# Gated cross attention on one core: the next chunk's summaries and row transposes placed ahead of the current chunk's output projection

## Chip, cores and metric

One core of a Trainium2 chip runs the whole program in one launch. The metric is the device time in microseconds. The kernel before was timed three times: 2039.60, 2035.11 and 2036.13 us, median 2036.13.

## What is computed

The program is a two-layer transformer over x of shape (8, 256, 512) with context of the same shape, float32. Four blocks follow each other: a gated long convolution, a routed mixture of experts, a gated linear cross attention, and a soft mixture of experts. The change lies in the third block alone. Cut to what matters, that block is:

```
q    = feature(layernorm(x) @ Wq.T)           # per head of 32 columns, 16 heads
gate = sigmoid(layernorm(x) @ Wg.T + bg)
k, v = split(ctx @ Wkv.T);  k = feature(k)    # feature(t) = t + 1 if t > 0 else exp(t)
kv   = sum over the 256 tokens of k^T v ;  k_sum = sum of k
attn = (q @ kv) / (q . k_sum + 1e-6)
x    = x + tanh(g) * ((attn * gate) @ Wo.T)
```

## The kernel before, in words

The 2048 tokens are cut into four chunks (NCH = 4) of 512 tokens. A chunk is four tiles of 128 tokens, and two batch entries of 256 tokens. Every float32 operand of a matmul is split into a float16 high part and a float16 low part, and one product is three matmuls (hi*hi, hi*lo, lo*hi), issued by `three` (L1470 to L1474). The work of a chunk c is cut into steps, each of which names the part that every engine plays in it:

- TC, TX (n = 0 to 3): TensorE transposes tile n of the context (TC) or of the normalised rows (TX) into a PSUM bank (L1478). ScalarE copies it out as the high part (L1304, L1310), VectorE makes the low part (L1406).
- CB: VectorE adds the two gathered expert rows to x (L1383, L1386) and takes the layer norm's statistics. NA is the variance and ScalarE's square root (L115), NB the reciprocal (L108) and the normalised rows (L1400).
- K, V: 12 matmuls of 512 columns each. For K, VectorE takes min(., 0) (L1368) and ScalarE the exponential (L1319). For V, ScalarE makes the high part (L1325), VectorE the low part (L1417). KF is the rest of K's feature: VectorE writes `feat` (L1375), ScalarE its high part (L1328), GpSimd its low part (L1281). GpSimd then issues the two gathers of tile n of chunk c + 1.
- Q, G, QF (n = 0 to 3): the same for the queries (L1331, L1344, L1286) and the gate (L1338, L1427), 12 matmuls each for Q and G.
- SM (n = 0 to 3): 12 matmuls each for the key-value summaries, out of all four K and V tiles of the chunk. TensorE waits for the low parts of all four (L1511). VectorE masks the sums (L1434). SS (n = 0, 1) splits them (L1347 on ScalarE, L1439 on VectorE).
- AT (n = 0 to 7): six matmuls of 256 columns. VectorE then takes denominator, reciprocal and product (L1447, L1450, L1455), ScalarE the high part (L1354), GpSimd the low part (L1290).
- OUT (n = 0 to 3): 12 matmuls, which wait for the low parts of AT 0 to 3 or AT 0 to 7 (L1533). VectorE adds the result to the rows (L1459), and SyncE stores them.

One list, `schedule`, holds the steps of all chunks in an order written out by hand (L1194 to L1200). Each of TensorE, VectorE, ScalarE and GpSimd walks this same list and plays its part of each step, so each engine's queue has the list's order, and a step that waits holds everything behind it on that engine. `mixed(a, b)` merges two lists evenly. In the kernel before the order for a chunk is: Q, G, QF of c mixed with TC, CB of c + 1; NA of c + 1; SM and SS of c; NB of c + 1; K, V, KF of c + 1 mixed with the eight AT of c; OUT of c mixed with TX of c + 1. The middle mix comes out as K0 AT0 V0 AT1 KF0, K1 AT2 V1 AT3 KF1, K2 AT4 V2 AT5 KF2, K3 AT6 V3 AT7 KF3. In front of the loop stand, for chunk 0, the transposes, the weights' splits (WS, L1314 and L1411), and K, V, KF mixed with WS and TX.

PSUM is a ring of eight banks, handed out in the list's order. A step that takes a bank waits until the step that used it eight uses earlier has been read (L1482 to L1486). SyncE's queue (L1221 to L1246) loads the context and the weights in eight pieces, then per chunk c: context and rows of c + 1, and then the four stores of chunk c, each behind its `out_read`.

Of the kernel before, what the change touches and what calls it, by code (L numbers as in the profile page):

```python
# [21 lines left out]
KD = D // P  # L22
CH = 4 * P
NCH = T // CH
# [27 lines left out]
def mixed(a, b):  # L52

    at = [((i + 0.5) / len(a), 0, o) for i, o in enumerate(a)] + [((i + 0.5) / len(b), 1, o) for i, o in enumerate(b)]
    return [o for _, _, o in sorted(at, key=lambda v: v[:2])]
# [1065 lines left out]
def xattn_phase(nc, k, x1s, y_rows, ctx, wq_t, wg_t, bg_cols, wkv_t, wo_t, x3):  # L1121
# [3 lines left out]
    with phase(nc) as st:  # L1125
# [8 lines left out]
        ctx_in, x2 = sb("a_ctx", [P, 4, D]), sb("a_x2", [P, X_BUFS, 4, D])  # L1134
# [20 lines left out]
        ctx_loaded, x_loaded = sem("a_ctx_loaded"), [sem(f"a_x_loaded{u}") for u in range(X_BUFS)]  # L1155
        y_loaded = [sem(f"a_y_loaded{u}") for u in range(4)]
        first_added, combined, normed = sem("a_first_added"), sem("a_combined"), sem("a_normed")
        c_turned, c_hi, c_lo = sem("a_c_turned"), sem("a_c_hi"), sem("a_c_lo")
        x_turned, x_hi, x_lo = sem("a_x_turned"), sem("a_x_hi"), sem("a_x_lo")
        k_done, v_done, q_done, g_done, gate_done = (sem(f"a_{n}") for n in ("k_done", "v_done", "q_done", "g_done", "gate_done"))  # L1160
        sum_done, mix_done, out_done, out_read = (sem(f"a_{n}") for n in ("sum_done", "mix_done", "out_done", "out_read"))
        v_hi_done, low_done, low_exp_done = sem("a_v_hi_done"), sem("a_low_done"), sem("a_low_exp_done")
        feat_done, feat_hi, feat_lo = sem("a_feat_done"), sem("a_feat_hi"), sem("a_feat_lo")
# [5 lines left out]
        x1s_d, x3_d, ctx_d = (a.rearrange("(c k p) d -> p (c k) d", p=P, k=4) for a in (x1s, x3, ctx))  # L1169
# [3 lines left out]
        NP = len(pieces)  # L1173

        def staged(n):
            cols = pieces[n][1][0].shape[2]
            return stage[:, n % 2, :, 0:cols]
# [6 lines left out]
        def ops(c, op, count):  # L1184
            return [(c, op, n) for n in range(count)] if c < NCH else []

        def projections(c, first, second, last, count):

            return [(c, op, n) for n in range(count) for op in (first, second, last)] if c < NCH else []

        def weights(first, end):
            return [(0, "WS", n) for n in range(first, end)]

        schedule = (ops(0, "TC", 4) + weights(0, 2) + ops(0, "CB", 4) + ops(0, "NA", 1) + ops(0, "NB", 1)  # L1194
                    + mixed(projections(0, "K", "V", "KF", 4), weights(2, 4) + ops(0, "TX", 4) + weights(4, NP)))
        for c in range(NCH):
            schedule += mixed(projections(c, "Q", "G", "QF", KD), [o for n in range(4) for o in ((c + 1, "TC", n), (c + 1, "CB", n)) if c + 1 < NCH])
            schedule += ops(c + 1, "NA", 1) + ops(c, "SM", 4) + ops(c, "SS", 2) + ops(c + 1, "NB", 1)
            schedule += mixed(projections(c + 1, "K", "V", "KF", 4), ops(c, "AT", 2 * KD))
            schedule += mixed(ops(c, "OUT", 4), ops(c + 1, "TX", 4))  # L1200


        READ = {"TC": (c_lo, 4), "TX": (x_lo, 4), "K": (feat_done, 8), "Q": (feat_done, 8), "V": (v_lo_done, 4), "G": (gate_exp, 4),
# [13 lines left out]
        def run(step):  # L1217
            for at in schedule:
                step(*at, home.get(at))

        @block.sync  # L1221
        def _(sp):
            def load_rows(c):
                if c >= X_BUFS:

                    sp.wait_ge(stored, (c - X_BUFS + 1) * 4 * 16)
                sp.dma_start(x2[:, c % X_BUFS], x1s_d[:, c * 4:c * 4 + 4, :]).then_inc(x_loaded[c % X_BUFS], 16)

            sp.dma_start(ctx_in[:, :, :], ctx_d[:, 0:4, :]).then_inc(ctx_loaded, 16)
            sp.dma_start(bg[:, :], bg_cols).then_inc(small_loaded, 16)  # L1230
            for n, (m, dst, b) in enumerate(pieces):
                if n >= 2:
                    sp.wait_ge(w_lo, n - 1)
                sp.dma_start(staged(n), m[b * P:(b + 2) * P, :].rearrange("(k p) n -> p k n", p=P)).then_inc(w_loaded[n % 2], 16)
                if n == 1:
                    load_rows(0)
            for c in range(NCH):
                if c < NCH - 1:

                    sp.wait_ge(c_turned, 4 * c + 4)  # L1240
                    sp.dma_start(ctx_in[:, :, :], ctx_d[:, c * 4 + 4:c * 4 + 8, :]).then_inc(ctx_loaded, 16)
                    load_rows(c + 1)
                for t in range(4):
                    sp.wait_ge(out_read, c * 4 + t + 1)
                    sp.dma_start(x3_d[:, c * 4 + t, :], x2[:, c % X_BUFS, t]).then_inc(stored, 16)
            sp.wait_ge(stored, NCH * 4 * 16)  # L1246
# [47 lines left out]
        @block.scalar  # L1294
        def _(act):
            A = nc.scalar.activation

            def step(c, op, n, bank):
                if op == "TC":
                    act.wait_ge(c_turned, c * 4 + n + 1)  # L1300
                    if c:

                        act.wait_ge(v_done, c * 4)
                    A(ct[0][:, :, n * P:(n + 1) * P], ring[:, bank, :].rearrange("p (k i) -> p k i", i=P), ACT.Copy).then_inc(c_hi, 1)  # L1304
                if op == "TX":
                    act.wait_ge(x_turned, c * 4 + n + 1)
                    if c:

                        act.wait_ge(g_done, c * 4)
                    A(xt[0][:, :, n * P:(n + 1) * P], ring[:, bank, :].rearrange("p (k i) -> p k i", i=P), ACT.Copy).then_inc(x_hi, 1)  # L1310
                if op == "WS":
                    act.wait_ge(w_loaded[n % 2], (n // 2 + 1) * 16)
                    _, dst, b = pieces[n]
                    A(dst[0][:, b:b + 2, :], staged(n), ACT.Copy).then_inc(w_hi, 1)  # L1314
                if op == "NA":
                    ln.root(nc, act, c)
                if op == "K":
                    act.wait_ge(low_done, c * 8 + n + 1)
                    A(low_exp[:, n % 2, :], low[:, n % 2, :], ACT.Exp).then_inc(low_exp_done, 1)  # L1319
                if op == "V":  # L1320
                    act.wait_ge(v_done, c * 4 + n + 1)
                    if c:

                        act.wait_ge(sum_done, c * 4)
                    A(v_hi[:, n, :, 0:P], ring[:, bank, :].rearrange("p (m i) -> p m i", i=P), ACT.Copy).then_inc(v_hi_done, 1)  # L1325
                if op == "KF":
                    act.wait_ge(feat_done, c * 8 + n + 1)
                    A(k_hi[:, n, :], feat[:, n % 2, :], ACT.Copy).then_inc(feat_hi, 1)  # L1328
                if op == "Q":
                    act.wait_ge(low_done, c * 8 + n + 5)  # L1330
                    A(low_exp[:, n % 2, :], low[:, n % 2, :], ACT.Exp).then_inc(low_exp_done, 1)  # L1331
                if op == "G":
                    act.wait_ge(g_done, c * 4 + n + 1)
                    if c:

                        act.wait_ge(denom_done, c * 8)

                    A(gate[:, n, :], ring[:, bank, :], ACT.Exp, bias=bg[:, n:n + 1], scale=-1.0).then_inc(gate_exp, 1)  # L1338
                if op == "QF":
                    act.wait_ge(feat_done, c * 8 + n + 5)  # L1340
                    if c:

                        act.wait_ge(mix_done, c * 8)
                    A(q_hi[:, n, :], feat[:, n % 2, :], ACT.Copy).then_inc(feat_hi, 1)  # L1344
                if op == "SS":
                    act.wait_ge(kv_done, c * 4 + n * 2 + 2)
                    A(kv_hi[:, n], kv[:, n], ACT.Copy).then_inc(kv_hi_done, 1)  # L1347
                if op == "AT":
                    b, m = divmod(n, KD)
                    act.wait_ge(weighted_done, c * 8 + n + 1)  # L1350
                    if c:

                        act.wait_ge(out_done, c * 4)
                    A(a_hi[:, m, b * N:(b + 1) * N], weighted[:, n % 2, :], ACT.Copy).then_inc(a_hi_done, 1)  # L1354
            act.wait_ge(small_loaded, 16)
            act.wait_ge(bg_negated, 1)
            run(step)

        @block.vector
# [107 lines left out]
        def _(pe):  # L1467
# [13 lines left out]
            def step(c, op, n, bank):  # L1481
# [26 lines left out]
                if op == "SM":  # L1508
# [5 lines left out]
                    for q in range(2):  # L1514
                        m = half * 2 + q
# [7 lines left out]
                if op == "AT":  # L1523

                    b, m = divmod(n, KD)
                    pe.wait_ge(feat_lo, c * 8 + 8)
                    pe.wait_ge(kv_lo_done, c * 2 + b + 1)
                    qs = [a[:, m, b * N:(b + 1) * N] for a in (q_hi, q_lo)]
                    for o in range(2):
                        last = three(ring[:, bank, o * N:(o + 1) * N], [a[:, b, m, o, :] for a in (kv_hi, kv_lo)], qs, True, True)  # L1530
                    last.then_inc(mix_done, 1)
                if op == "OUT":
                    pe.wait_ge(a_lo_done, c * 8 + (n // 2 + 1) * 4)  # L1533
                    pe.wait_ge(w_lo, NP)
                    for m in range(KD):
                        last = three(ring[:, bank, :], [a[:, m, n * P:(n + 1) * P] for a in (a_hi, a_lo)],
                                     [a[:, m, :] for a in wo], m == 0, m == KD - 1)
                    last.then_inc(out_done, 1)
            run(step)


# [686 lines left out]
```

## Time and profile before

| | us |
|---|---|
| median of three runs (2035.11 to 2039.60) | 2036.13 |
| the profiled execution's own time | 2038.1 |
| its span, first to last instruction | 2036.3 |
| cross attention in it, first transpose to last output matmul | 832.1 to 1173.6 |
| mean granted TensorE clock over the span | 0.924 |

The span is the time from the first to the last instruction, and the profiled execution's own time has about 2 us around it. All starts in the rows further down are microseconds from the start of the span. A group of 12 matmuls is shown as 12 overlapping rows: a row's duration (0.38 us for 512 columns) is longer than the distance between two starts (about 0.22 us), since matmuls are pipelined. The granted clock is a share of full speed, where 1.00 is 2.4 GHz and 0.50 is 1.2 GHz.

### The profile page before, as it was taken

How to read it: one execution, taken by the hardware profiler on the slowest of the kernel's cores; microseconds unless marked ns; L12 is line 12 of the kernel's file. 1: busy time of each engine (PE TensorE's matmuls, PEld its weight loads, DVE VectorE, ACT ScalarE, POOL GpSimd, SP SyncE). 2: the span in 40 equal slices, each digit the busy share in tenths (PEclk: the TensorE clock that was granted, in tenths of full speed). 3: DMA queues.
4: the chain of work that ended last, by engine and by line, in shares of the span. 5: the costliest groups of instructions: out<-in, count | busy, mean ns of one | idle time of the engine just before them, and what ended most of it. 6: DMA issues, size and time to landing. Idle time of an engine off the chain costs nothing. (4 is left out here: it accounts for less than half of the span.)

```text
span 2036.3 us, 29066 instructions
## 1 busy us (share of the span) xinstructions
PE 1699.5 (83%) x10248; PEld 1006.8 (49%) x10249; DVE 1141.6 (56%) x2234; ACT 716.2 (35%) x1366; POOL 419.4 (21%) x324
## 2 busy tenths in 40 slices
PE   2989948999279999588988736798989898989898
PEld 2778823444146666344544413454545454545454
DVE  4978843332643333576868646646465655556463
ACT  2322113333222222242333225735454443535352
POOL 1323303333411110233222113501010101010100
PEclk6999979999689999789999868899999899999999
DMA  8222233333422222433020052200000000000000
GB/s 179 62 74 86 86 119 107 119 119 99 134 68 84 82 82 68 185 104 103 13 92 21 11 176 66 90 1 32 1 32 0 31 0 31 0 31 0 21 13 20
DMA packets 78734, 134.52 MB, mean 66 GB/s; under 512 B 6626, under 2 KB 31202, under 8 KB 78514
## 3 DMA queue, kind: packets, MB, share of 16 engines
q1 hardware_dynamic: 71488, 113.45, 17.4%
q0 software_dynamic: 5680, 18.62, 3.2%
q10 hardware_dynamic: 1474, 1.21, 0.2%
q8 instruction: 59, 0.97, 0.2%
q14 instruction: 33, 0.27, 0.0%
HBM read 101.98 MB, written 31.28 MB: 65 GB/s over the span
## 5 line engine op out<-in xcount | busy, mean ns | idle before, releaser
L2041 PE MATMUL s_ring<-w_mu_hi,s_xt_hi 128*128 128x512 f16 x256 | 104.7, 409 | 45.7 <-DVE s_xt_lo L1948 45.7
L1953 DVE TENSOR_REDUCE s_top<-s_lg 128x1 f32<-128x512 f32 x64 | 43.8, 685 | 130.5 <-ACT s_lg L1855 130.5
L463 PE MATMUL ring<-prod_hi,toep 128*128 128x288 f16 x320 | 93.0, 291 | 18.2 <-DVE terms L383 10.1
L274 POOL TENSOR_TENSOR prod_lo<-prod,prod_hi 128x2304 f16<-128x2304 f32 x16 | 73.2, 4576 | 166.9 <-ACT prod_hi L307 156.6
L2025 DVE TENSOR_TENSOR s_g_lo<-s_ring,s_g_hi 128x512 f16<-128x512 f32 x64 | 43.4, 689 | 109.9 <-ACT s_g_hi L1897 109.9
L2042 PE MATMUL s_ring<-w_mu_lo,s_xt_hi 128*128 128x512 f16 x256 | 104.4, 408 | 0.0
L2043 PE MATMUL s_ring<-w_mu_hi,s_xt_lo 128*128 128x512 f16 x256 | 103.8, 405 | 0.0
L1800 POOL TENSOR_TENSOR s_h_lo<-s_h,s_h_hi 128x512 f16<-128x512 f32 x32 | 36.9, 1154 | 311.7 <-DVE s_h_hi L2022 311.7
L1794 POOL TENSOR_TENSOR s_xln<-s_xln,s_gamma 128x512 f32<-128x512 f32 x16 | 21.7, 1376 | 372.2 <-DVE s_xln L1934 372.2
L2041 PE MATMUL s_ring<-w_w_hi,s_xt_hi 128*128 128x512 f16 x256 | 98.0, 383 | 0.0
L2042 PE MATMUL s_ring<-w_w_lo,s_xt_hi 128*128 128x512 f16 x256 | 98.0, 383 | 0.0
L2043 PE MATMUL s_ring<-w_w_hi,s_xt_lo 128*128 128x512 f16 x256 | 97.8, 382 | 0.0
L2041 PE MATMUL s_acc<-w_w_hi,s_g_hi 128*128 128x512 f16 x256 | 97.1, 379 | 0.0
L2042 PE MATMUL s_acc<-w_w_lo,s_g_hi 128*128 128x512 f16 x256 | 97.0, 379 | 0.0
L2043 PE MATMUL s_acc<-w_w_hi,s_g_lo 128*128 128x512 f16 x256 | 97.0, 379 | 0.0
L464 PE MATMUL ring<-prod_lo,toep 128*128 128x288 f16 x320 | 93.0, 291 | 0.0
L465 PE MATMUL ring<-prod_hi,toep 128*128 128x288 f16 x320 | 93.0, 290 | 0.0
L2006 DVE TENSOR_TENSOR s_xw_lo<-s_ring,s_xw_hi 128x512 f16<-128x512 f32 x64 | 44.1, 689 | 73.0 <-ACT s_xw_hi L1889 73.0
L1855 ACT ACTIVATE s_lg<-s_ring,s_rs 128x512 f32<-128x512 f32 x64 | 44.0, 688 | 115.8 <-PE s_ring L2043 115.8
L380 DVE TENSOR_TENSOR terms<-ring,q_e 128x512 f32<-128x512 f32 x64 | 66.8, 1044 | 27.3 <-PE ring L465 25.0
L1087 DVE TENSOR_TENSOR e_h<-e_up,e_silu 128x352 f32<-128x352 f32 x39 | 20.4, 524 | 109.3 <-ACT e_silu L1066 109.3
L991 POOL DMA_INDIRECT e_rows<-normed_rows,slot_token x39 | 37.0, 950 | 197.6 <-PE e_turn L1005 181.7
(396 smaller groups left out, 4919.2 us busy)
## 6 DMA issues: line engine op xcount, KB each, us to landing
expert_rows<-e_y SPq DMA_DIRECT2D x39, 256.0 KB, 2.0
toep<-ssm_split SPq DMA_DIRECT2D x14, 512.0 KB, 5.1
stage<-in_L_ffn_gate_w SPq DMA_DIRECT2D x8, 704.0 KB
stage<-in_L_ffn_up_w SPq DMA_DIRECT2D x8, 704.0 KB
c_rows<-in_ctx SPq DMA_DIRECT2D x8, 512.0 KB, 10.3
x_rows<-in_x SPq DMA_DIRECT2D x8, 512.0 KB
res<-in_x SPq DMA_DIRECT2D x128, 32.0 KB
after_conv<-gated SPq DMA_DIRECT2D x128, 32.0 KB
```

Of the source, the lines that this page charges most:

```text
L274: nc.gpsimd.tensor_tensor(prod_lo[:, u].rearrange("p k e r -> p (k e r)"), prod[:, u, :], prod_hi[:, u].rearrange("p k e r -> p (k e r)"), ...
L380: nc.vector.tensor_tensor(to(0, (9, 4), (1, 8)), values(0, (8, 4), (1, 8)), weights(0, (0, 4), (1, 8)), ALU.mult)
L463: nc.tensor.matmul(out, w_hi, hi, start=(n == 0), stop=False)
L464: nc.tensor.matmul(out, w_hi, lo, start=False, stop=False)
L465: last = nc.tensor.matmul(out, w_lo, hi, start=False, stop=(n == m))
L1855: A(lg[:, t, j * D:(j + 1) * D], ring[:, bank, :], ACT.Copy, scale=rs[:, t:t + 1]).then_inc(S["lg_out"], 1)
L1953: V.tensor_reduce(top[:, t, j:j + 1], lg[:, t, j * D:(j + 1) * D], AX.X, ALU.max).then_inc(S["top_done"], 1)
L2006: V.tensor_tensor(xw[1][:, t, j * D:(j + 1) * D], ring[:, bank, :], xw[0][:, t, j * D:(j + 1) * D], ALU.subtract).then_inc(S["xw_lo"], 1)
L2025: V.tensor_tensor(g[1][:, n % G_BUFS, :], ring[:, bank, :], g[0][:, n % G_BUFS, :], ALU.subtract).then_inc(S["g_lo"], 1)
L2041: mm(out_, a[0], b_[0], start=first, stop=False)
L2042: mm(out_, a[0], b_[1], start=False, stop=False)
L2043: return mm(out_, a[1], b_[0], start=False, stop=last_)
```

## The change

The steps are the same and so are the instructions of each. What differs is their order in the list, two waits, and SyncE's order.

- For chunk 0, SM and SS stand in front of the loop, behind K, V, KF, where they stood behind Q, G, QF of chunk 0.
- In the loop, behind Q, G, QF of c, come NA, K0, V0 and NB of c + 1. Then the other ten steps of K, V, KF of c + 1 are mixed with AT of c. This comes out as KF0 AT0, K1 AT1 V1 AT2 KF1 AT3, K2 V2 AT4 KF2 AT5, K3 AT6 V3 AT7 KF3. Then SM 0 to 3, TX 0 to 3 and SS 0, 1 of c + 1, and last OUT 0 to 3 of c.
- In the last chunk the order behind Q, G, QF is AT0 to AT4, OUT0, AT5, AT6, OUT1, AT7, OUT2, OUT3.
- TensorE's wait of AT asks for the low part of its own column block of the queries and no longer for all four. ScalarE's SS waits until the AT steps of the chunk before have read the summaries.
- SyncE issues the loads of context and rows of chunk c + 2 ahead of the stores of chunk c. Those of chunk 1 stand where they stood, behind the weights.

```diff
         schedule = (ops(0, "TC", 4) + weights(0, 2) + ops(0, "CB", 4) + ops(0, "NA", 1) + ops(0, "NB", 1)
-                    + mixed(projections(0, "K", "V", "KF", 4), weights(2, 4) + ops(0, "TX", 4) + weights(4, NP)))
+                    + mixed(projections(0, "K", "V", "KF", 4), weights(2, 4) + ops(0, "TX", 4) + weights(4, NP))
+                    + ops(0, "SM", 4) + ops(0, "SS", 2))
         for c in range(NCH):
             schedule += mixed(projections(c, "Q", "G", "QF", KD), [o for n in range(4) for o in ((c + 1, "TC", n), (c + 1, "CB", n)) if c + 1 < NCH])
-            schedule += ops(c + 1, "NA", 1) + ops(c, "SM", 4) + ops(c, "SS", 2) + ops(c + 1, "NB", 1)
-            schedule += mixed(projections(c + 1, "K", "V", "KF", 4), ops(c, "AT", 2 * KD))
-            schedule += mixed(ops(c, "OUT", 4), ops(c + 1, "TX", 4))
+            if c + 1 < NCH:
+                schedule += ops(c + 1, "NA", 1) + projections(c + 1, "K", "V", "KF", 4)[:2] + ops(c + 1, "NB", 1)
+                schedule += mixed(projections(c + 1, "K", "V", "KF", 4)[2:], ops(c, "AT", 2 * KD))
+                schedule += ops(c + 1, "SM", 4) + ops(c + 1, "TX", 4) + ops(c + 1, "SS", 2) + ops(c, "OUT", 4)
+            else:
+                at, out = ops(c, "AT", 2 * KD), ops(c, "OUT", 4)
+                schedule += at[:KD] + mixed(at[KD:], out[:2]) + out[2:]
...
+            def load_chunk(c):
+                sp.wait_ge(c_turned, 4 * c)
+                sp.dma_start(ctx_in[:, :, :], ctx_d[:, c * 4:c * 4 + 4, :]).then_inc(ctx_loaded, 16)
+                load_rows(c)
+
+            load_chunk(1)
             for c in range(NCH):
-                if c < NCH - 1:
-
-                    sp.wait_ge(c_turned, 4 * c + 4)
-                    sp.dma_start(ctx_in[:, :, :], ctx_d[:, c * 4 + 4:c * 4 + 8, :]).then_inc(ctx_loaded, 16)
-                    load_rows(c + 1)
+                if c + 2 < NCH:
+                    load_chunk(c + 2)
...
                 if op == "SS":
                     act.wait_ge(kv_done, c * 4 + n * 2 + 2)
+                    if c:
+
+                        act.wait_ge(mix_done, c * 8)
...
                 if op == "AT":
 
                     b, m = divmod(n, KD)
-                    pe.wait_ge(feat_lo, c * 8 + 8)
+                    pe.wait_ge(feat_lo, c * 8 + 4 + m + 1)
                     pe.wait_ge(kv_lo_done, c * 2 + b + 1)
```

## Rows read from the trace of the kernel before

**Rows 1.** Timeline, TensorE: start us, us, engine, line, op, out<-in, count, [idle before <-releaser]
```profile
906.90 0.27 PE L1519 MATMUL a_ring<-a_v_hi,a_k_hi 128*128 128x256 f16 x1
...
960.20 0.38 PE L1472 MATMUL a_ring<-a_xt_hi,wq_hi 128*128 128x512 f16 x1 [1.46 <-issue]
...
965.64 0.87 PE L1478 MATMUL a_ring<-ident,a_ctx 128*128 128x128 f32 x3 [2.69 <-DMA a_ctx<-in_ctx]
...
986.88 0.27 PE L1519 MATMUL a_ring<-a_v_hi,a_k_hi 128*128 128x256 f16 x1
...
991.27 0.38 PE L1472 MATMUL a_ring<-wkv_hi,a_ct_hi 128*128 128x512 f16 x1
...
1022.17 0.39 PE L1472 MATMUL a_ring<-wo_hi,a_a_hi 128*128 128x512 f16 x1 [1.34 <-DVE a_feat L1375]
...
1025.21 0.38 PE L1472 MATMUL a_ring<-wo_hi,a_a_hi 128*128 128x512 f16 x1
...
1030.82 0.38 PE L1472 MATMUL a_ring<-wo_hi,a_a_hi 128*128 128x512 f16 x1 [2.42 <-DVE a_feat L1375]
...
1038.49 0.38 PE L1472 MATMUL a_ring<-a_xt_hi,wq_hi 128*128 128x512 f16 x1 [1.46 <-issue]
...
1116.57 0.38 PE L1472 MATMUL a_ring<-a_xt_hi,wq_hi 128*128 128x512 f16 x1 [1.46 <-issue]
...
1137.28 0.27 PE L1519 MATMUL a_ring<-a_v_hi,a_k_hi 128*128 128x256 f16 x1
```

**Rows 2.** Timeline, VectorE, chunk 1 after its last gate group, same columns
```profile
990.32 1.00 DVE L104 TENSOR_TENSOR x_var<-x_gap,x_spread 128x4 f32<-128x4 f32 x1
...
995.98 0.17 DVE L108 RECIPROCAL x_rstd<-x_std 128x4 f32<-128x4 f32 x1
...
998.62 0.42 DVE L1447 SCALAR_TENSOR_TENSOR a_denom<-a_ring,a_gate 128x256 f32<-128x256 f32 x1
...
1002.24 0.69 DVE L1417 TENSOR_TENSOR a_v_lo<-a_ring,a_v_hi 128x512 f16<-128x512 f32 x1 [0.97 <-ACT a_v_hi L1325]
...
1029.44 0.68 DVE L1375 SCALAR_TENSOR_TENSOR a_feat<-a_ring,a_low_exp 128x512 f32<-128x512 f32 x1
```

**Rows 3.** Timeline, ScalarE, same stretch and columns
```profile
991.36 0.20 ACT L115 ACTIVATE x_std<-x_var 128x4 f32<-128x4 f32 x1
...
994.82 1.28 ACT L1319 ACT_TABLE_LOAD   x1
...
1001.63 0.58 ACT L1325 ACTIVATE a_v_hi<-a_ring 128x512 f16<-128x512 f32 x1
```

**Rows 4.** Timeline, GpSimd, chunk 1, last K tile
```profile
1030.86 1.16 POOL L1281 TENSOR_TENSOR a_k_lo<-a_feat,a_k_hi 128x512 f16<-128x512 f32 x1
```

**Rows 5.** Timeline, GpSimd and TensorE, before the first Q and G groups end
```profile
883.88 1.16 POOL L1281 TENSOR_TENSOR a_k_lo<-a_feat,a_k_hi 128x512 f16<-128x512 f32 x1 [5.54 <-ACT a_k_hi L1328]
...
884.21 0.66 PE L1478 MATMUL a_ring<-ident,a_ctx 128*128 128x128 f32 x2 [7.44 <-DMA a_ctx<-in_ctx]
```

**Rows 6.** Windows: PE, PEld, DVE, ACT, POOL busy us (count), PEclk, DMA share, GB/s
```profile
832.10:834.50 2.40, 2.35 (x11) 2.35 (x12) 0.65 (x2) 0.94 (x2) 1.79 (x3) 0.50 1.02 418
...
835.20:836.00 0.80, 0.41 (x3) 0.17 (x2) 0.64 (x2) 0.76 (x2) 0.66 (x1) 0.96 1.03 415
...
884.20:890.00 5.80, 5.79 (x16) 2.59 (x17) 3.48 (x5) 0.80 (x2) 2.75 (x3) 0.51 0.65 219
...
1156.50:1159.60 3.10, 3.09 (x8) 1.14 (x9) 3.03 (x4) 0.42 (x1) 0.67 (x1) 0.51 0.00 0
```

**Rows 7.** Timeline, VectorE, GpSimd and TensorE, last chunk
```profile
1144.83 0.42 DVE L1447 SCALAR_TENSOR_TENSOR a_denom<-a_ring,a_gate 128x256 f32<-128x256 f32 x1
...
1147.41 0.41 DVE L1447 SCALAR_TENSOR_TENSOR a_denom<-a_ring,a_gate 128x256 f32<-128x256 f32 x1
...
1148.02 0.67 POOL L1290 TENSOR_TENSOR a_a_lo<-a_mixed,a_a_hi 128x256 f16<-128x256 f32 x1 [8.10 <-ACT a_a_hi L1354]
...
1173.22 0.38 PE L1474 MATMUL a_ring<-wo_hi,a_a_lo 128*128 128x512 f16 x1
```
## The prediction

> **What bounds the kernel now.** I read the page first, then the timelines of TensorE and VectorE over the cross attention, and last the windows for the granted clock. TensorE's timeline [rows 1] shows a repeating period: from Q0 of one chunk to Q0 of the next are 960.20 to 1038.49 = 78.3 us and 1038.49 to 1116.57 = 78.1 us. Small waits stand in it: 2.69 us for the context (its load is queued behind the stores), 1.34 us before OUT0, 2.42 before OUT2, 1.46 before Q0. Most name VectorE. VectorE's timeline [rows 2] shows why. From its first AT (998.62) to KF3 (1029.44) it needs 30.8 us for 8 AT, 4 V, 3 K and 3 KF (KF0 to KF2), and idles only where V waits for ScalarE's copy, 0.97 us each. TensorE's same stretch, K0 to OUT0, is 991.27 to 1022.17, 30.9 us with its waits inside [rows 1]. So between the last G and the last low part VectorE sets the pace. TensorE hides two OUT and two TX groups under VectorE's last steps (OUT0 starts 7.3 us before KF3's feature), and only 1038.49 - 1030.82 = 7.7 us of the chunk follow when AT7 is ready.
>
> **Chunks 1 to 3 in the new order.** I walk the list from the first instant after G3 (986.88 in chunk 1 [rows 1]), called G.
> - SM leaves this place: 991.27 - 986.88 = 4.4 us of TensorE, the mask and split of VectorE too. But VectorE's next steps are K0, V0, NB, KF0, and they wait for ScalarE. The square root starts at 991.36 and takes 0.20 [rows 3], behind VectorE's variance [rows 2]; nothing moves it. The table load behind it takes 1.28 [rows 3], so K0's exponential starts at G + 6.0. That pass and V0's copy take about 0.6 each (the copy's row has 0.58 [rows 3]), V0's low part starts at G + 7.2 and takes about 0.6 [rows 2]. NB and one 512-column pass took 998.62 - 995.98 = 2.64 [rows 2]; NB and KF0 take as much. So the first AT starts on VectorE at G + 10.5, where it started at 998.62 - 986.88 = G + 11.7. Thus 4.4 us less work in front is worth 1.2 us.
> - From the first AT to KF3's feature: 30.8, less V0 (0.97 + 0.6) and KF0 (0.6) already done, plus about 0.3 because V2 now follows K2 directly and ScalarE must make exponential and copy in turn. That is 28.9 us, so KF3's feature starts at G + 39.4. AT's relaxed wait on TensorE buys nothing, as VectorE reaches each AT later than TensorE.
> - SM of the next chunk now waits for KF3's low part: GpSimd starts it 1.42 us behind the feature (1029.44 to 1030.86 [rows 2, 4]) and takes 1.16 [rows 4]. **SM starts at G + 42.1.** TensorE has finished AT7 by G + 30.9 (the K0 to OUT0 stretch of before, waits and all), so it idles over 11 us, at one place, with four TX and two ready OUT groups queued behind SM.
> - After it TensorE still has SM 4.4 us, and four OUT and four TX, 1025.21 - 1022.17 = 3.04 us a pair [rows 1], 12.2 us. VectorE has little to do then, so nothing else waits.
> - The clock: before OUT0 of the last chunk TensorE idled over 7 us and then ran at a granted 0.51 (1.2 GHz) for 3.1 us; after a like wait for the context the low stretch was 5.8 us [rows 6]. Half of the low time is lost: 1.55 to 2.9 us. For 11 to 13 us of idling I take 2.1 us, nearer the last chunk's because no transfer or PSUM wait is mixed in; the ends are 0 (the clock happens to be up) and 2.9.
>
> G to the next Q0 is then 42.1 + 4.4 + 12.2 + 2.1 = 60.8 us. Q0 to G3 is 20.7 us without transposes (1116.57 to 1137.28 [rows 1]) and four TC add 4 x 0.45 (a pair less an eighth of 20.7), 22.5 us in all. The context load of chunks 2 and 3 stands ahead of the stores and needs only TC3 of the chunk before, some 60 us earlier, so its wait goes entirely, with the low clock behind it. SyncE's moved row load of chunk 3 waits for chunk 0's stores, long done; the 32 gathers of GpSimd keep their places behind KF, and KF3's stand behind the low part that SM needs.
>
> Sums: chunk 0's G to Q0 was 53.3 (906.90 to 960.20 [rows 1]), now 60.8: **+7.5**. The two full periods were 78.3 and 78.1, now 83.3: **+5.0 and +5.2**.
>
> **Chunk 0 in front of the loop.** SM(0) must wait for KF3(0)'s low part, 883.88 + 1.16 [rows 5]: start 885.1. Before, Q0 had run inside the 7.44 us wait for the context, whose place in SyncE's queue is unchanged, TC0 started at 884.21 [rows 5] and G0 ended at 890.0, all at 0.51 [rows 6]. Now SM 4.4 + 2.1 for the clock, Q0 2.6, TC0 0.45 and G0 2.6 end at 897.2: **+7.2**.
>
> **The last chunk.** Without SM and SS in front, VectorE's first AT starts at about G + 1.3 (when the gate of QF3 is done), 1138.6 for 1144.83 [rows 7]. Each AT takes 1147.41 - 1144.83 = 2.58, and its low part ends 3.86 after its start (1148.02 + 0.67 - 1144.83 [rows 7]). OUT0 starts at 1138.6 + 3 x 2.58 + 3.86 = 1150.2, at the low clock, and ends at 1154.4. VectorE, in order, waits for it from 1151.5, so interleaving costs 3.1 us there. With OUT0's and OUT1's pass (0.65 each) AT7 starts at 1161.0, its low part ends at 1164.9, and OUT2, OUT3 (5.2 + 1.55 for the clock) end at 1171.6 instead of 1173.6 [rows 7]: **-2.0**.
>
> Total: 7.5 + 5.0 + 5.2 + 7.2 - 2.0 = **+22.9 us**. The soft mixture behind it is only shifted. The profiled execution would take 2038.1 + 22.9 = 2061.0; it lay 2.0 above the median of 2036.13, so I predict 2059.0. Its own range: with the clock up at all four SM starts 8.4 less, with 2.9 at each 3.2 more, and 1 us either way for each of the four starts: 2046.6 to 2066.2.
>
> **A rule against this change.** Transposes now stand in a block of 16 between SM and OUT. In this trace 16 transposes alone ran at 0.50, and at 835.2, with nothing else behind or beside them, the granted clock was 0.96 [rows 6]: transposes raised it. The Trainium skill says the opposite (TensorE: Matmul & The Clock Gate, Part 4: PE-mode transpose): the full clock does not engage for transposes, since they do not count as busy in the same way. This trace disagrees with it. I keep it as a rival.
>
> **The rivals.**
> - Transposes do not hold the clock: OUT0 behind the TX block runs at 1.2 GHz too, 2.6 us more for each of three blocks, 2059.0 + 7.8 = 2066.8. Against it is the row at 835.2. Chance 0.07.
> - The change does not do what it says for the loads: the contexts come no sooner, because the early load collides with something on SyncE's queue. The 22.5 us become 26.6 again (78.3 less 51.6, 1038.49 - 986.88): 2 x 4.1 = 8.2, 2067.2. Nothing in the trace speaks for it. Chance 0.06.
> - The VectorE chain closes up: K0 and V0's reload wait (2.6 us) and the three V waits (3.2 us) vanish because ScalarE is less often behind. 3 x 5.8 = 17.4 us less, with the clock's low end 4 x 0.55 less again: 2039.4, within 0.2%. Against it: ScalarE's place in the chain is fixed by the list. Chance 0.07.
> - Faster: TensorE and not VectorE sets the pace in the K, V, AT stretch, and VectorE's lateness is only an echo of the waits now removed. Then SM starts 1.42 + 1.16 behind the stretch of at most 30.9, at G + 33.5, 8.6 us earlier in three chunks, and without the long idle the clock stays up (3 x 2.1): 2059.0 - 25.8 - 6.3 = 2026.9. It decides from the point where SM starts before about G + 36.6 ((22.9 - 6.3) / 3 = 5.5 us sooner than reckoned). For it: TensorE's waits of 1.34, 2.42 and 1.46 us go [rows 1]. Against it: VectorE idles only 4 x 0.97 in 30.8 us. Chance 0.06.
>
> **How the numbers follow.** My forecast has 0.74, those four 0.26. A measurement of this kernel can tell about 0.2% (4.1 us) from no change. Slower by more: 0.74 + 0.07 + 0.06 = 0.87; within: 0.07; faster: 0.06. The range 2045 to 2069 takes the forecast's bounds and the two slower rivals and leaves out 0.13 and a little of the edges.
>
> **What would show it.** In the changed trace: TensorE idle of 11 to 14 us in front of SM's first matmul in each of chunks 1 to 3, and some 11 us in front of the first of all at 885, released by GpSimd's low part or VectorE's feature; SM at a granted 0.5; no wait for the context but the first; KF3's feature at G + 39.4; Q0 to Q0 of 83 us; last OUT 2 us nearer to its G. The prediction is wrong if the idle before SM is under 5 us, or if VectorE's stretch from first AT to KF3 is clearly shorter than 28.9 us.

## The result and the profile after

The changed kernel took 2059.86 us (median of 4 runs, 2057.78 to 2063.56), the kernel before beside it 2037.87 us (4 runs, 2035.11 to 2039.68). The ratio is 1.0105, with a 95% interval of 1.0079 to 1.0132: slower by 22.0 us in the medians. The prediction was 2059.0, in a range of 2045 to 2069. The profiled execution of the changed kernel took 2061.15 us, its span is 2059.4.

The code in front of the cross attention is the same in all kernels here, and yet the first context transpose started anywhere from 832.0 to 840.0 us of the span in the profiles of this study. So I also compare **the stage**: from the start of the first context transpose to the end of the last output matmul. Before, it was 832.15 to 1173.6, 341.5 us. After, the first transpose is at 834.07 and the last matmul ends at 1198.99 (the row of [rows 7] has become 1198.61 + 0.38), 364.9 us. The stage grew by 23.4 us, and that is the whole loss: the rest of the span moved by less (1.9 us more ahead of the stage, 2.3 us less behind it).

The timeline of TensorE in the changed kernel, in the columns of [rows 1]. In order of time: the first context transpose; SM of chunk 0 and Q0 behind it; the first step behind G3 of chunk 0, then SM of chunk 1 and Q0 of chunk 1; the same three for the next chunk; Q0 of chunk 3; and in the last chunk the first AT behind G3 (1163.62), OUT0, OUT2 and the last OUT matmul.

```profile
834.07 0.48 PE L1489 MATMUL a_ring<-ident,a_ctx 128*128 128x128 f32 x1 [9.42 <-DMA a_ctx<-in_ctx]
...
887.48 0.37 PE L1530 MATMUL a_ring<-a_v_hi,a_k_hi 128*128 128x256 f16 x1 [10.89 <-POOL a_k_lo L1289]
...
894.29 0.38 PE L1483 MATMUL a_ring<-a_xt_hi,wq_hi 128*128 128x512 f16 x1
...
916.76 0.38 PE L1483 MATMUL a_ring<-wkv_hi,a_ct_hi 128*128 128x512 f16 x1
...
958.83 0.37 PE L1530 MATMUL a_ring<-a_v_hi,a_k_hi 128*128 128x256 f16 x1 [13.43 <-POOL a_k_lo L1289]
...
977.91 0.38 PE L1483 MATMUL a_ring<-a_xt_hi,wq_hi 128*128 128x512 f16 x1
...
1000.38 0.38 PE L1483 MATMUL a_ring<-wkv_hi,a_ct_hi 128*128 128x512 f16 x1
...
1042.23 0.37 PE L1530 MATMUL a_ring<-a_v_hi,a_k_hi 128*128 128x256 f16 x1 [11.74 <-POOL a_k_lo L1289]
...
1060.59 0.38 PE L1483 MATMUL a_ring<-a_xt_hi,wq_hi 128*128 128x512 f16 x1
...
1142.90 0.38 PE L1483 MATMUL a_ring<-a_xt_hi,wq_hi 128*128 128x512 f16 x1
...
1163.62 0.27 PE L1483 MATMUL a_ring<-a_q_hi,a_kv_hi 128*128 128x256 f16 x1
...
1176.57 0.58 PE L1483 MATMUL a_ring<-wo_hi,a_a_hi 128*128 128x512 f16 x1 [8.75 <-issue]
...
1191.09 0.58 PE L1483 MATMUL a_ring<-wo_hi,a_a_hi 128*128 128x512 f16 x1 [5.92 <-issue]
...
1198.61 0.38 PE L1485 MATMUL a_ring<-wo_hi,a_a_lo 128*128 128x512 f16 x1
```

The small waits of [rows 1] (1.34, 2.42, 1.46 us) and the waits for the second and third context are gone. In their place stands one long wait per chunk in front of SM, 13.43 and 11.74 us here, released by the low part that GpSimd makes of the last K tile. The view of TensorE's waits over the stage adds them up:

```profile
PE a_ring L1530 <- POOL a_k_lo L1289: 47.8, 4, 13.4
PE a_ring L1483 <- issue: 15.3, 3, 8.7
PE a_ring L1489 <- DMA a_ctx<-in_ctx: 9.4, 1, 9.4
...
PE a_ring L1483 <- DVE a_feat L1386: 6.6, 3, 2.3
```

The columns are the sum in us, the number of waits and the longest. Of the stage's 364.9 us TensorE spent 47.8 in front of the four SM. The only context wait left is that of the very first one. Three waits of 2.1 to 2.35 us for VectorE stand in the middle of the K, V, AT stretch (6.6 us): TensorE is ahead of VectorE there already. The same stretch on VectorE, ScalarE and GpSimd, behind G3 of chunk 1 (G = 1000.38), answers to [rows 2 to 4]:

```profile
1007.52 0.69 DVE L1428 TENSOR_TENSOR a_v_lo<-a_ring,a_v_hi 128x512 f16<-128x512 f32 x1 [2.10 <-ACT a_v_hi L1333]
1008.13 0.17 DVE L108 RECIPROCAL x_rstd<-x_std 128x4 f32<-128x4 f32 x1
...
1010.76 0.41 DVE L1458 SCALAR_TENSOR_TENSOR a_denom<-a_ring,a_gate 128x256 f32<-128x256 f32 x1
...
1039.56 0.68 DVE L1386 SCALAR_TENSOR_TENSOR a_feat<-a_ring,a_low_exp 128x512 f32<-128x512 f32 x1
```

```profile
1005.08 1.28 ACT L1327 ACT_TABLE_LOAD   x1
1006.37 0.63 ACT L1327 ACTIVATE a_low_exp<-a_low 128x512 f32<-128x512 f32 x1
1006.91 0.58 ACT L1333 ACTIVATE a_v_hi<-a_ring 128x512 f16<-128x512 f32 x1
```

```profile
1040.98 1.15 POOL L1289 TENSOR_TENSOR a_k_lo<-a_feat,a_k_hi 128x512 f16<-128x512 f32 x1
```

V0's low part waits 2.10 us for ScalarE, whose table load and two passes stand ahead of it. The first AT starts on VectorE at G + 10.4, KF3's feature at G + 39.2, the low part ends at 1042.13, and SM starts at G + 41.85. Last the windows of SM, TX and OUT behind that wait, in the columns of [rows 6]:

```profile
1042.20:1048.50 6.30, 6.26 (x49) 5.20 (x50) 2.08 (x3) 0.00 (x0) 1.91 (x2) 0.69 0.32 86
1048.50:1050.30 1.80, 1.80 (x19) 1.79 (x18) 1.24 (x2) 1.18 (x3) 0.00 (x0) 1.00 0.00 0
1050.30:1060.60 10.30, 10.30 (x50) 4.61 (x49) 6.38 (x9) 2.77 (x4) 0.00 (x0) 1.00 0.20 78
```

SM takes 6.3 us at a mean granted clock of 0.69, where it took 4.4 before (991.27 - 986.88 in [rows 1]). The 16 transposes and the OUT block behind it run at 1.00.

### The profile page after: what moved, and what is told of

The parts are those of the page before. It is cut to its first block and busy times, and to the rows that moved or that the text cites. A ratio compares the mean times of both kernels' runs of the same rounds, so it can differ in the third digit from the quotient of the medians.

```text
span 2059.4 us, 29072 instructions
## 1 busy us (share of the span) xinstructions
PE 1699.6 (83%) x10248; PEld 1009.9 (49%) x10249; DVE 1143.8 (56%) x2234; ACT 715.2 (35%) x1366; POOL 418.2 (20%) x324
```

## The experiments

Each kernel was run beside the kernel before on the same chip. "Stage" is the length defined above, from the kernel's profile: 341.5 us before, 364.9 changed. Three groups were run, each on a chip of its own. Those with SM behind OUT, the filler of 44, the loads alone and AT's wait are compared with the kernel before at 2039.01 us (17 runs). The two with V's low part moved, the loads undone and the first SM are compared with 2038.75 (13 runs), and the filler of 55 and the last chunk with 2036.53 (9 runs). The changed kernel's own 1.0105 is against 2037.87. So kernels of different groups are better compared by their ratios than by their medians. There is one profile of each kernel, and it need not be a typical execution: that of the loads with V's low part moved is the fastest of its four runs (2012.44, median 2016.34), that of the change with V's low part moved the slowest of its eight (2049.93, median 2045.71).

**The place of SM.** The changed kernel, SM and SS behind OUT and TX:

```diff
-                schedule += ops(c + 1, "SM", 4) + ops(c + 1, "TX", 4) + ops(c + 1, "SS", 2) + ops(c, "OUT", 4)
+                schedule += mixed(ops(c, "OUT", 4), ops(c + 1, "TX", 4)) + ops(c + 1, "SM", 4) + ops(c + 1, "SS", 2)
```

> The changed kernel with SM and SS of the next chunk behind OUT and TX, which are mixed as in the kernel before. Theory V: TensorE does two OUT and two TX groups while VectorE finishes its AT, OUT2 starts behind the low part of AT7 at G + 40.5, SM ends at about G + 51, and G to the next Q0 falls from 60.2 to 61.1 us to about 51.5: 3 x 9 = 27 us faster than the changed kernel, about 2033. Rival B (what costs is that TensorE now runs K0, V0 and NB ahead of AT, or that V2 follows K2, and not where SM stands): at most 3 us faster than the changed kernel, about 2057.

It took 2040.02 us (12 runs, ratio to before 1.0007, 0.9995 to 1.0019). The stage is 342.1 us, 22.8 less than changed and 0.6 more than before. G to Q0 is 52.9, 52.9 and 52.8 us. Its rows on TensorE in chunk 0 (G = 917.28):

```profile
946.83 0.39 PE L1483 MATMUL a_ring<-wo_hi,a_a_hi 128*128 128x512 f16 x1 [0.90 <-DVE a_feat L1386]
...
958.06 0.38 PE L1483 MATMUL a_ring<-wo_hi,a_a_hi 128*128 128x512 f16 x1 [5.01 <-DVE a_feat L1386]
...
965.80 0.27 PE L1530 MATMUL a_ring<-a_v_hi,a_k_hi 128*128 128x256 f16 x1
```

Theory V holds and rival B falls: with all else of the change in place, the two lists in another order give back 22.8 us, as much as was lost. The expectation had 27 us and a time of 2033. OUT2 starts at G + 40.8 (40.5 expected), but it took 4.3 us (to the transpose at 962.3) behind that 5.01 us idle, at a mean granted clock of 0.62, where a full-clock group takes 2.6. That covers the 1.4 us per chunk by which 52.9 misses 51.5. That the kernel ends level with the kernel before is a sum of two other terms of the change: the stretch up to the G of chunk 0 is still 7.6 us longer (82.3 for 74.7), and the two Q0 to G are 8.2 us shorter in all.

**The clock.** The changed kernel with matmuls that nobody reads in front of SM, 44 in each chunk, and then 55 in chunks 1 to 3 (the edit shown):

```diff
                     b, half = divmod(n, 2)
+                    if n == 0:
+                        for r in range(55 if c else 44):
+                            mm(ring[:, bank, :], wkv[0][:, 0, 0:P], wkv[0][:, 0, 0:D], start=True, stop=True)
                     pe.wait_ge(feat_lo, c * 8 + 4)
```

> The changed kernel with 44 matmuls of 512 columns added in front of each chunk's SM (some 9.5 us of TensorE), into the PSUM bank that SM0 then overwrites, so that TensorE is busy where it idled. The output is unchanged. Theory V: SM starts at the same instant, at a granted 1.00; the four SM blocks take 4.4 us each instead of 6.8, 7.0, 6.3 and 5.9, so about 8 us faster than the changed kernel, about 2052. Rival C (the low clock is most of the 23 us lost): 15 us or more faster, 2045 or less.

> The filler with 55 instead of 44 matmuls in chunks 1 to 3, which closes the 2.8 us that TensorE still idled in front of SM. Theory V: the four SM blocks take 4.4 us each (two of them took 5.9 and 5.7), SM starts at the same instants, so 2 to 3 us faster than with the filler of 44, about 2053, and still 14 us or more slower than the kernel before: the idle time and not its clock is the loss. Rival C (clock): 2045 or less.

With 44 in every chunk: 2055.47 us (6 runs, ratio 1.0083, 1.0067 to 1.0099), stage 359.4. With 55 in chunks 1 to 3: 2052.89 us (4 runs, ratio 1.0082, 1.0063 to 1.0100), stage 357.2. The windows in front of the last SM and over it in the kernel with 44, and over the last three SM in the kernel with 55:

```profile
1112.00:1115.50 3.50, 3.50 (x17) 1.37 (x14) 2.94 (x4) 0.46 (x1) 0.67 (x1) 1.00 0.00 0
1115.50:1118.30 2.80, 0.00 (x0) 0.00 (x0) 0.85 (x2) 1.05 (x2) 1.82 (x2) 0.88 0.00 0
1118.30:1124.20 5.90, 5.89 (x50) 5.04 (x51) 2.08 (x3) 0.00 (x0) 0.00 (x0) 0.77 0.00 0
```

```profile
954.30:958.70 4.40, 4.40 (x49) 4.04 (x49) 2.08 (x3) 0.00 (x0) 1.91 (x2) 1.00 0.43 118
1035.10:1039.50 4.40, 4.40 (x48) 4.05 (x49) 2.08 (x3) 0.00 (x0) 1.91 (x2) 1.00 0.42 118
1115.90:1120.30 4.40, 4.40 (x50) 4.05 (x50) 2.07 (x3) 0.00 (x0) 0.00 (x0) 1.00 0.02 4
```

With TensorE busy until SM may start, all four SM take 4.4 us at 1.00, 8.4 us less than in the changed kernel, and the stage is 7.7 us shorter (the last chunk, which the edit leaves alone, took 1.2 us more). That is the clock's share of the 23.4: a third. Rival C falls, since the other 15.7 us stay. The first expectation was a little too high (5.5 us in the stage where 8 were expected): twice the clock fell within the 2.8 us that TensorE still idled, and those SM took 5.9 and 5.7 us. By the ratios both fillers gained some 4.5 us on the changed kernel (1.0083 and 1.0082 for 1.0105), with intervals that overlap: the 7.7 us, and the step from 44 to 55, stand in the profiles alone.

**VectorE's chain.** V's low part one AT later in VectorE's order, V0's behind NB, in the changed kernel and in the kernel before with the new order of loads. The instruction is the same; only its place on VectorE moves:

```diff
+        spread_out, due = [], []
+        for at in schedule:
+            spread_out.append(at)
+            if at[1] == "V":
+                due.append((at[0], "VL", at[2]))
+            if due and (at[0] == 0 and at[1] == "V" or at[1] in ("AT", "NB")):
+                spread_out += due
+                due = []
+        schedule = spread_out
-        SECOND = {"KF": "K", "QF": "Q"}
+        SECOND = {"KF": "K", "QF": "Q", "VL": "V"}
...
-                if op == "V":
+                if op == "VL":
                     dve.wait_ge(v_hi_done, c * 4 + n + 1)
```

> The changed kernel with V's low part on VectorE (same instruction) placed one AT later in the list than ScalarE's copy (V0's behind NB), so that VectorE does not wait for the copy: 2.10, 0.97, 1.18 and 0.97 us a chunk. Theory V: KF3 and with it SM move up by their sum, 5.2 us, in three chunks: SM at G + 36.6 instead of 41.8, 15.6 us faster than the changed kernel, about 2044. Rival P (SM's start is set by TensorE's own stretch or by GpSimd's gathers): SM moves by less than 1 us and the time stays at 2058 to 2060.

> The kernel before with the changed order of the loads and V's low part one AT later, as above. Theory V: with SM in its old place the 4 x 0.97 us of VectorE in each K, V, AT stretch go straight to the end of the chunk: G to Q0 47.7 instead of 51.6, three times, 11.6 us faster than with the loads alone (2030.95), about 2019. Rival P: no more than 2 us faster than with the loads alone.

On top of the change: 2045.71 us (8 runs, ratio 1.0033, 1.0020 to 1.0046), stage 351.2, 13.7 less than changed. SM starts at 1032.91, with G at 996.49:

```profile
996.49 0.38 PE L1492 MATMUL a_ring<-wkv_hi,a_ct_hi 128*128 128x512 f16 x1
...
1032.91 0.37 PE L1539 MATMUL a_ring<-a_v_hi,a_k_hi 128*128 128x256 f16 x1 [10.29 <-POOL a_k_lo L1298]
```

That is G + 36.4, where 36.6 was expected and 41.85 stood before the edit. VectorE's four waits for ScalarE's copy (2.10, 0.97, 1.18 and 0.97 us) are gone from its timeline. SM's start follows VectorE's chain as it was reckoned, though not one instruction of TensorE or GpSimd was moved. Rival P falls. The stage gained 13.7 and not 15.6 us. SM alone took 7.2, 6.5, 7.0 and 7.2 us here against 6.8, 7.0, 6.3 and 5.9, 1.9 us more in all, which is the clock again, and the last chunk took 1.1 us more.

With SM in its old place and the loads early: 2016.34 us (4 runs, ratio 0.9893, 0.9872 to 0.9914), stage 314.4. **This version beats both kernels**, the kernel before by 1.1%. Against the loads alone it gained 14.6 us in the medians (about 13 by the ratios, as the chips differ) and 20.2 in the stage, more than the 11.6 expected. G to Q0 is 46.8 us in all three chunks (47.7 expected, from a base of 51.6). With the loads alone it had been 53.3, 53.1 and 51.6, because in the first two the clock fell behind OUT2's idle. That is gone too: OUT2 waits 0.77 us, where it waited 2.42 [rows 1]. These three make 17.6 of the 20.2 us, and the stretches ahead of the first G and behind the last 1.3 each. The stage overstates the gain: the two profiled executions are 19.9 us apart, the medians 14.6. The chunk in which the clock did not fall in either kernel gives the share of VectorE's chain, 51.6 to 46.8, so 4.8 us for the 3.9 expected and some 14.5 in three chunks. The other 3 us of the three are low clock that the one profile had and the other had not.

```profile
1018.35 0.38 PE L1484 MATMUL a_ring<-wo_hi,a_a_hi 128*128 128x512 f16 x1 [0.77 <-DVE a_feat L1387]
...
1026.02 0.38 PE L1484 MATMUL a_ring<-a_xt_hi,wq_hi 128*128 128x512 f16 x1 [1.46 <-issue]
```

**The loads.** The new order of loads in the kernel before, and the old order in the changed kernel:

```diff
+            load_chunk(1)
             for c in range(NCH):
-                if c < NCH - 1:
-
-                    sp.wait_ge(c_turned, 4 * c + 4)
-                    sp.dma_start(ctx_in[:, :, :], ctx_d[:, c * 4 + 4:c * 4 + 8, :]).then_inc(ctx_loaded, 16)
-                    load_rows(c + 1)
+                if c + 2 < NCH:
+                    load_chunk(c + 2)
```

> The kernel before with the changed order of SyncE's loads alone. Theory V (VectorE's stretch from the first AT to KF3 and the place of SM behind it explain the loss; the loads are a gain inside it): the waits for the contexts of chunks 2 and 3 (2.69 and 2.12 us) and the low clock behind them go, each Q0 to G3 takes 22.5 us instead of 26.6, 6 to 8 us faster than the kernel before (about 2030). Rival L (the earlier loads collide with other transfers and give nothing): no change, within 2 us of the kernel before.

> The changed kernel with SyncE's order of before. Theory V: the loads of chunks 2 and 3 are again issued behind OUT3's store, so TC0 of chunks 1 and 2 waits 2 to 3 us more and runs at the low clock: Q0 to G 26.5 instead of 22.5 in two chunks, 8 us slower than the changed kernel, about 2068. Rival L: the order of the loads makes no difference beside the new order of steps, within 1 us in the stage.

Alone, the loads gave 2030.95 us (6 runs, ratio 0.9958, 0.9943 to 0.9973), stage 334.6, 6.9 less than before, with Q0 to G 22.5 us twice. Rival L falls. Undone in the changed kernel they cost twice what was expected: 2073.99 us (4 runs, ratio 1.0169, 1.0147 to 1.0191), stage 380.8, 15.9 more than changed.

```profile
982.78 0.66 PE L1486 MATMUL a_ring<-ident,a_ctx 128*128 128x128 f32 x2 [4.92 <-DMA a_ctx<-in_ctx]
...
1071.89 0.66 PE L1486 MATMUL a_ring<-ident,a_ctx 128*128 128x128 f32 x2 [4.02 <-DMA a_ctx<-in_ctx]
```

```profile
976.46 0.43 SPq L1246 DMA_DIRECT2D a_ctx<-in_ctx  x1
```

```profile
976.00:982.70 6.70, 1.86 (x9) 0.66 (x7) 0.75 (x2) 0.63 (x1) 0.00 (x0) 0.93 0.85 269
982.80:990.00 7.20, 7.20 (x23) 3.25 (x24) 3.88 (x6) 1.73 (x3) 0.00 (x0) 0.60 0.19 74
```

In the order of before, Q0 had stood 1.46 us behind OUT3 for the last row transpose [rows 1]. In the new order it starts at once (975.1 here), so the same load, issued behind OUT3's store, is later relative to Q0: the wait is 4.92 where it was 2.69, and the clock then has a mean of 0.60 for 7.2 us. The loads' new place is thus worth 7 us to the old order and 16 to the new one.

**The first SM.** SM and SS of chunk 0 behind Q0 and TC0 instead of in front of the loop:

```diff
-                    + ops(0, "SM", 4) + ops(0, "SS", 2))
+                    )
         for c in range(NCH):
-            schedule += mixed(projections(c, "Q", "G", "QF", KD), [o for n in range(4) for o in ((c + 1, "TC", n), (c + 1, "CB", n)) if c + 1 < NCH])
+            part = mixed(projections(c, "Q", "G", "QF", KD), [o for n in range(4) for o in ((c + 1, "TC", n), (c + 1, "CB", n)) if c + 1 < NCH])
+            schedule += part[:2] + (ops(0, "SM", 4) + ops(0, "SS", 2) if c == 0 else []) + part[2:]
```

> The changed kernel with SM and SS of chunk 0 two steps later, behind Q0 and TC0 of the first mix. Theory V: Q0 runs in the wait for the context again, SM starts at about the same instant (885 to 888) behind it, and G0 ends 2.6 to 3 us sooner: 3 us faster than the changed kernel, about 2057. Rival: SM(0) in front costs nothing by itself, because the context's wait ends at the same instant: no difference in the stage's length.

It took 2058.78 us (4 runs, ratio 1.0096, 1.0070 to 1.0122). The stage is 361.5, 3.4 less than changed: 3.8 less by the end of chunk 0's G3 (78.9 us behind the first transpose against 82.7), and 0.4 more behind it. Of the 3.8 us 1.4 are the clock's, as SM took 5.4 us here and 6.8 there. The profile shows the expected 3 us. The runs alone could not tell it.

**The last chunk.** AT 0 to 7 and then OUT 0 to 3, in the changed kernel:

```diff
-                schedule += at[:KD] + mixed(at[KD:], out[:2]) + out[2:]
+                schedule += at + out
```

> The changed kernel with the last chunk's order as in the kernel before (AT 0 to 7, then OUT 0 to 3), and all else as changed. Theory V: VectorE no longer stands at OUT0 while TensorE works on it, the low part of AT7 is ready at about G + 23.2 instead of 27.5, and the stage ends at G + 30 to 31 instead of 35.4: 4 to 5 us faster than the changed kernel, about 2055. Rival I (interleaving OUT0 and OUT1 hides them under AT): 2 us or more slower than the changed kernel.

It took 2060.19 us (5 runs, ratio 1.0113, 1.0095 to 1.0131). The expected gain of 4 to 5 us does not show in the runs, and they are too few to exclude it. The stage is 360.7, 4.2 less, 3.8 of it behind the last G3: 31.6 us to the end for 35.4. Rival I falls in the stage: interleaving costs. Here OUT2 starts 23.3 us behind the last G3 (23.2 expected), where it started at 1191.09 - 1163.62 = 27.5. Most of the 4.2 us between them is one wait of VectorE in the changed kernel:

```profile
1180.66 0.75 DVE L1470 SCALAR_TENSOR_TENSOR a_x<-a_ring,tanh_gates,a_x 128x512 f32<-128x512 f32 x1 [2.80 <-PE a_ring L1485]
```

VectorE stands 2.80 us at OUT0 while TensorE works on it, with three AT queued behind, and its passes for OUT0 and OUT1 (0.75 us here) stand ahead of AT7 as well. That the time did not follow is an open point: in this kernel's profile the stage began 2.9 us later than in the changed kernel's, in code that is the same.

**AT's wait.** The changed kernel with the wait of before:

```diff
-                    pe.wait_ge(feat_lo, c * 8 + 4 + m + 1)
+                    pe.wait_ge(feat_lo, c * 8 + 8)
```

> The changed kernel with AT's wait of before on TensorE (low parts of all four column blocks of the queries). Theory V: VectorE reaches AT0 only at G + 10.4, so the relaxed wait buys nothing: within 1 us of the changed kernel, 2060. Rival: TensorE's head start counts, 2 us or more slower than the changed kernel.

It took 2066.99 us (4 runs, ratio 1.0128, 1.0108 to 1.0148), and the stage is 367.8, 2.9 more. The expectation failed. In chunks 0 to 2 nothing moved (G to Q0 61.1, 60.2 and 59.8 us, as changed). In the last chunk, where AT0 stands directly behind G3, TensorE waits:

```profile
1172.04 0.27 PE L1483 MATMUL a_ring<-a_q_hi,a_kv_hi 128*128 128x256 f16 x1 [2.57 <-issue]
```

VectorE follows at once there, so the 2.57 us go into the end. The median is 7.1 us above the changed kernel's, by the ratios 4.7, and the two intervals overlap. What goes beyond the 2.9 us is not in the stage: this profile's stage began at 840.0, 5.9 us later, in code that is the same. Whether it is more than scatter the runs do not show.

## Why the prediction was right

The total came within 1 us of the forecast, and by its own steps, as the two profiles show. That it was so close is in part luck: the terms are off by up to 1.1 us each, and the misses nearly cancel.

| step | predicted | measured | from |
|---|---|---|---|
| chunk 0 in front of the loop | +7.2 | +7.9 | first transpose to the G of chunk 0: 906.90 - 832.15 = 74.8, now 916.76 - 834.07 = 82.7 |
| chunk 0, G to Q0 | +7.5 | +7.8 | 53.3 to 977.91 - 916.76 = 61.1 |
| Q0 to Q0, chunk 1 | +5.0 | +4.4 | 78.3 to 1060.59 - 977.91 = 82.7 |
| Q0 to Q0, chunk 2 | +5.2 | +4.2 | 78.1 to 1142.90 - 1060.59 = 82.3 |
| last chunk, G to end | -2.0 | -0.9 | 36.3 to 1198.99 - 1163.62 = 35.4 |
| sum | +22.9 | +23.4 | |

- **SM behind KF3's low part** was the step that carried the sum: start at G + 42.1 predicted, 41.85 measured. Its parts hold one by one: first AT at G + 10.5 (10.4), KF3's feature at G + 39.4 (39.2; with the 1.42 and 1.16 us behind it the prediction's own terms give 42.0, not 42.1), and the 1.42 us from there to GpSimd is unchanged (1039.56 to 1040.98). That VectorE's chain and nothing else sets it was an argument in the prediction. The edit of V's low part, which shortens that chain alone, and the edit that moves SM show it.
- **The low clock** was put at 2.1 us for each SM. The four took 6.8, 7.0, 6.3 and 5.9 us, 8.4 over 4 x 4.4 in all: 2.1 each on average, inside the bounds of 0 and 2.9. The filler confirms the size (8.4 us over the four SM). That the average fell on 2.1 is luck: single SM cost 1.5 to 2.6 us, and the same four cost 1.9 us more in the kernel with V's low part moved. The sign "SM at a granted 0.5" came only in part: the means over the four SM are 0.62 to 0.74, as the clock rose again within them.
- **The loads** of chunks 2 and 3: 4.2 and 4.0 us were taken off, and Q0 to G is 22.5 us as said. As a judgment on the edit this was too small. It compares with the waits of the old order; in the new one, without this edit, the waits would have been longer.
- **The last chunk** is the term that was mis-sized most, by 1.1 us: the start of OUT2 was right (G + 27.6, measured 27.5), but OUT2 and OUT3 took 7.9 us and not 6.75. I had put one low stretch of 3.1 us on them from [rows 6], and it was longer. That the interleaving costs VectorE 3.1 us at OUT0 was right (2.80), and the run with the plain order shows that the gain of the last chunk came in spite of it.
- **AT's wait.** "AT's relaxed wait on TensorE buys nothing" holds for the chunks it was said of. For the last chunk the prediction used the early AT0 without noting that it hangs on this very edit, and the expectation of the run then forgot it.
- **The rivals.** The rival that transposes do not hold the clock did not come: the window of the 16 transposes and that of OUT behind them show 1.00. As a test of the Trainium skill's statement (TensorE: Matmul & The Clock Gate, Part 4: PE-mode transpose) this is weak, since the block took 1.8 us and SM had raised the clock before. The stronger one is the first block of the stage, where the changed kernel's trace disagrees with the statement as that of before does: 16 transposes at 0.50 behind 9.42 us of idling, and then 1.00 though nothing else ran on TensorE. The windows:

```profile
834.07:837.70 3.63, 3.63 (x16) 3.28 (x16) 1.70 (x4) 1.79 (x3) 2.71 (x4) 0.50 1.02 410
838.00:839.50 1.50, 0.00 (x0) 0.00 (x0) 0.94 (x2) 1.50 (x2) 1.04 (x2) 1.00 1.02 415
```

  The loads did come early. TensorE did not set the pace: it ran ahead and then idled 11.7 to 13.4 us. VectorE's chain did not close up: its waits for ScalarE's copy stayed (2.10, 0.97, 1.18 and 0.97 us).

So the change lost time by its central move. It takes 4.4 us of SM from a place where they were partly hidden (worth 1.2 us to VectorE's chain), and puts them, with TX and all four OUT behind them, after the last link of VectorE's chain, where TensorE has nothing to overlap with.

## What to carry to other kernels

When engines walk one list in order, a step is not free where its own engine idles. Ask which engine's chain sets that stretch and what becomes queued behind the step's wait: here the summaries waited for the last link, and work that was ready stood behind them. Look for gain in the chain itself: four waits of about 1 us on the pacing engine, removed by moving one instruction past its neighbour, together with two loads moved ahead of stores, gave 1.1%. And where an effect is smaller than the scatter of whole runs, compare one stage by fixed marks in the profiles, and say that the runs alone do not show it.

## What the runs showed of the hardware beyond that

- TensorE's clock fell after waits as short as 2.1 to 2.8 us. In front of the last SM of the filler kernel the granted clock had already a mean of 0.88 over the idle 2.8 us, and SM then ran at 0.77. In front of another SM of the same kernel the same idle did nothing (4.4 us). In the changed kernel a wait of 2.13 us in chunk 2 was followed by 0.50, while after 2.35 us at the same place in chunk 0 the clock stayed at 1.00. A short idle has a price only sometimes. The rows of the 2.13 us:

```profile
1104.17 0.39 PE L1483 MATMUL a_ring<-a_q_hi,a_kv_hi 128*128 128x256 f16 x1 [2.13 <-DVE a_feat L1386]
```

```profile
1104.20:1107.50 3.30, 3.30 (x11) 1.57 (x12) 3.02 (x4) 1.17 (x3) 1.94 (x3) 0.50 0.00 0
```
- A four-column addition on VectorE took 1.00 us, in both kernels, while GpSimd ran a subtraction. The same instruction took 0.16 us in chunk 0, at 856.14 of the changed kernel, with nothing on GpSimd. The rows of the changed kernel:

```profile
1003.83 1.00 DVE L104 TENSOR_TENSOR x_var<-x_gap,x_spread 128x4 f32<-128x4 f32 x1
```

```profile
1003.62 1.18 POOL L1294 TENSOR_TENSOR a_q_lo<-a_feat,a_q_hi 128x512 f16<-128x512 f32 x1 [4.46 <-ACT a_q_hi L1352]
```

```profile
856.14 0.16 DVE L104 TENSOR_TENSOR x_var<-x_gap,x_spread 128x4 f32<-128x4 f32 x1
```

  VectorE's instruction ends at 1004.83, as GpSimd's does at 1004.80. The Trainium skill (SBUF — State Buffer, Who interferes with whom) says that a VectorE instruction with two SBUF inputs contends with a GpSimd instruction that reads SBUF, and calls the contention on the shared ports an exclusive lock. The trace agrees: 0.16 us of work took until the other's end. It holds throughout: in the profiles of the twelve kernels all 36 of these additions beside a GpSimd instruction took 1.00 us, and all 108 with none beside them 0.16 or 0.17. No run was made to vary it.
